# Two starting columns of the time shift written by GpSimd instead of VectorE, in a fused RWKV, attention and FP4 kernel

## The chip, the cores and the metric

The kernel runs on one core of one Trainium2 chip. The metric is the device time in microseconds (us) of one execution, as the median of several. The names in the profile are PE for TensorE (PEld is its weight load), DVE for VectorE, ACT for ScalarE, POOL for GpSimd and SP for the queue that issues the DMAs.

## The reference

The input x has 16 sequences of 512 tokens with 128 channels. Four parts are applied in a row, each on a layer norm of x and added to x: a stack of four RWKV layers, a gated FFN with FP4 quantised inputs and weights, a causal attention with one head of 64, and the same FFN again. The change lies in the RWKV layers:

```
for l in range(4):
    h = layernorm(x, ln1_w[l], ln1_b[l]);  hh = time_shift(h)
    k, v, sr = (mixes of h and hh) @ Wk, Wv, sigmoid(... @ Wr)
    x = x + (sr * wkv(time_decay, time_first, k, v)) @ Wo
    h = layernorm(x, ln2_w[l], ln2_b[l])
    hh = time_shift(h)                       # token t sees token t - 1, token 0 sees zeros
    xk = h * cmk[l] + hh * (1 - cmk[l])
    xr = h * cmr[l] + hh * (1 - cmr[l])
    x = x + sigmoid(xr @ Wcr) * (square(relu(xk @ Wck)) @ Wcv)
```

## The kernel before, in words

One sequence in one layer is a round: round r is layer r // 16 and sequence r % 16, and there are 64. Channels lie on the 128 partitions and the 512 tokens along the row, save for the layer norms, where 128 tokens lie on the partitions in four chunks. A round passes through some fifteen stages on five engines. Each engine has its own program, written as a loop over ticks; in tick t it works on the stages of several rounds, in an order that is written out by hand, and semaphores join the engines. In the steady part each engine does one piece of some fifteen rounds in one tick. The engines' ticks are not aligned in time: the tick numbers of two engines say nothing on which runs first.

The second time shift, of `h` after `ln2`, is built so. PE turns the normalised chunks (`turn2`, L1076), ACT writes `past`, the shifted term with its bias, for tokens 1 to 511 of both mixes (`keep_past`, L891), and DVE adds the unshifted term (`mix_k`, L420, and `mix_r`, L428). Column 0 of `past` has no token before it and depends on the layer alone; it is copied from the small tensor `cp`. `past` has two buffers, so the copy is made only in the first two rounds of each layer (`r % NB < 2`), 8 times in all, by `first_past` (L413). `mix_k` waits for it by the semaphore `pads`.

What stands around it: on DVE, in the order of the program, `scan_bb` (L374), `scan_aa` (L382), `gate` (L435), `sub_d` (L356), `variances` (L318, L319), `first_past`, `mix_k`, `mix_r`, in some rounds the preparation of a layer's weights (L253, L254), `mix_rt` (L332), `mix_v` (L339), `mix_t` (L325). The last three read two tensors in SBUF each. On POOL: `add_nd` (L692), `add_xb` (L708), `arg_r` (L685), `norm1_rest` (L659, three chunks of 128 columns), `rsqrts` (L651, a power, and L653, a product), `mul_y` (L697), `norm2_rest` (L659 again). On ACT, `tanh_c` (L912) waits for `add_xb`, and later in the tick `exp_d` (L853) writes what `scan_bb` reads.

Of the kernel before, what the change touches and what calls it, by code (L numbers as in the profile page):

```python
# [8 lines left out]
ALU = mybir.AluOpType  # L9
# [3 lines left out]
L, NB, T, C, F, I, D = 4, 16, 512, 128, 512, 352, 64  # L13
NT = T // 128
NR = L * NB
# [61 lines left out]
def hybrid_program(nc, x_in, weights, vecs, rows, fp4w, qkv, wout, mask, ident, out):  # L77
    ctx = ExitStack()
    with ctx:
# [28 lines left out]
        cw, cp, cz = [sb(k, [128, 2, L]) for k in ("cw", "cp", "cz")]  # L108
# [114 lines left out]
        def vector():  # L223
# [182 lines left out]
                    w.wait_ge(xa_done, r + 1)  # L406
                    stats(n_2, r, X[r % NB])

            def first_past(r):
                if 0 <= r < NR and r % NB < 2:  # L410
                    w.wait_ge(vecs_done, VECS)
                    w.wait_ge(xm_done, 2 * r - 2)
                    e.tensor_scalar(past[r % 2][:, :, 0:1], cp[:, :, r // NB:r // NB + 1], 1.0, 0.0, ALU.mult, ALU.add).then_inc(pads, 1)  # L413

            def mix_k(r):
                if 0 <= r < NR:
                    w.wait_ge(past_done, r + 1)
# [131 lines left out]
            for t in range(FIRST, TICKS):  # L549
                bn1(t - 1)  # L550
                add_xa(t - 7)
                mul_vs(t - 5)
                scan_bb(t - 5)
                scan_aa(t - 5)
                gate(t - 11)
                a_add(att_job(t - 6))
                scan_pp(t - 4)
                rwkv(t - 6)
                mul_up(ffn_job(t - 4), 0)
                fx_add(ffn_job(t - 2))  # L560
                mul_up(ffn_job(t - 4), 1)
                sub_d(t - 4)
                fx_sub(ffn_job(t - 2))
                fh_add(ffn_job(t - 5), 0)
                mul_up(ffn_job(t - 4), 2)
                fh_sub(ffn_job(t - 5), 0)
                bn2(t - 7)
                gated(t - 5)
                variances(t - 1)
                fx_scale(ffn_job(t - 1))  # L570
                mul_up(ffn_job(t - 4), 3)
                first_past(t - 8)
                init_stats(t + 1)
                mix_k(t - 8)
                mix_r(t - 8)
                prepare(t - 1)
                a_mask(att_job(t - 4), 0)
                fx_inverse(ffn_job(t - 1))
                fh_max(ffn_job(t - 4))
                a_max(att_job(t - 4), 0)  # L580
                weights_scales(t - 2)
                fh_scale(ffn_job(t - 4))
                fh_add(ffn_job(t - 5), 1)
                fh_inverse(ffn_job(t - 4))
                mix_rt(t - 3)
                init_affine(t)
                weights_rounded(t - 3)
                fh_sub(ffn_job(t - 5), 1)
                a_inverse(att_job(t - 5))
                a_mask(att_job(t - 4), 1)  # L590
                a_max(att_job(t - 4), 1)
                a_mask(att_job(t - 4), 2)
                a_max(att_job(t - 4), 2)
                mix_v(t - 3)
                mix_t(t - 3)
                a_mask(att_job(t - 4), 3)
                a_max(att_job(t - 4), 3)
                a_bn(att_job(t))
                f_bn(ffn_job(t + 3))
                fx_max(ffn_job(t))  # L600

        def gpsimd():
# [30 lines left out]
            def weights_divided(u):  # L633
                if u == 0:
                    w.wait_ge(q_steps, 3)
                    e.tensor_tensor(blocks(qw), blocks(qw), spread(wsc[:, 0, :], NQ // 16), ALU.mult).then_inc(q_y, 1)
# [25 lines left out]
            def norm1_rest(r):  # L662
                if 0 <= r < NR:
                    w.wait_ge(turned1, r - 1)
                    normalise(n_1, r, X[r % NB], z1[r % 2], 1, z1_rest)
# [33 lines left out]
            def scaled_p(r):  # L699
                if 0 <= r < NR:  # L700
                    w.wait_ge(p_done, r + 1)
                    w.wait_ge(seed_done, r + 1)
                    e.tensor_tensor(p[r % 2][:, :], p[r % 2][:, :], rc[r % 2][:, :], ALU.mult).then_inc(ps_done, 1)

            def add_xb(r):
                if 0 <= r < NR:
                    w.wait_ge(gate_done, r + 1)
                    e.tensor_tensor(X[r % NB][:, :], X[r % NB][:, :], cr[r % 2][:, :], ALU.add).then_inc(x_done, 1)  # L708
# [47 lines left out]
            for t in range(FIRST, TICKS):  # L756
                fx_divided(ffn_job(t - 4))
                scaled_p(t - 8)
                sub_dh1(t - 5)
                add_res(ffn_job(t + 1))  # L760
                fh_divided(ffn_job(t - 7), 0)
                fh_scaled(ffn_job(t - 8), 1)
                fh_divided(ffn_job(t - 7), 1)
                add_nd(t - 7)
                a_rsqrt(att_job(t - 3))
                add_xb(t - 13)
                arg_r(t - 6)
                f_rsqrt(ffn_job(t - 1))
                weights_divided(t - 5)
                norm1_rest(t - 4)  # L770
                fh_scaled(ffn_job(t - 7), 0)
                init_rsqrt(t - 1)
                fx_scaled(ffn_job(t - 4))
                rsqrts(t - 3)
                mul_y(t - 7)
                weights_scaled(t - 5)
                norm2_rest(t - 9)
                add_bias(att_job(t - 6))
# [649 lines left out]
```

## Time and profile before

| | us |
|---|---|
| median of 3 runs | 1329.43 (1328.66 to 1329.69) |
| profiled execution | 1329.69 |
| its span, first to last instruction | 1328.3 |
| PE busy | 1260.3 (95%) |
| DVE busy | 1221.2 (92%) |
| ACT busy | 1203.7 (91%) |
| POOL busy | 1170.1 (88%) |

The clock granted to TensorE is 0.993 of full speed in the mean. The RWKV layers take the span up to about 850 us, and the FFN and the attention what follows. A row of the timeline gives the start in us from the start of the span, the duration, the engine, the line, the operation with out<-in, how many instructions are merged (x3), and in brackets the idle time before it and what ended it. Starts are given to a hundredth of a microsecond; on one engine the next instruction starts up to 0.1 us before the recorded end of the one before it, so the distance from start to start is what an instruction takes of the engine.

### The profile page before, as it was taken

How to read it: one execution, taken by the hardware profiler on the slowest of the kernel's cores; microseconds unless marked ns; L12 is line 12 of the kernel's file. 1: busy time of each engine (PE TensorE's matmuls, PEld its weight loads, DVE VectorE, ACT ScalarE, POOL GpSimd, SP SyncE). 2: the span in 40 equal slices, each digit the busy share in tenths (PEclk: the TensorE clock that was granted, in tenths of full speed). 3: DMA queues.
4: the chain of work that ended last, by engine and by line, in shares of the span. 5: the costliest groups of instructions: out<-in, count | busy, mean ns of one | idle time of the engine just before them, and what ended most of it. 6: DMA issues, size and time to landing. Idle time of an engine off the chain costs nothing.

```text
span 1328.3 us, 23258 instructions
## 1 busy us (share of the span) xinstructions
PE 1260.3 (95%) x7177; PEld 919.8 (69%) x7177; DVE 1221.2 (92%) x2177; ACT 1203.7 (91%) x2283; POOL 1170.1 (88%) x1391
## 2 busy tenths in 40 slices
PE   2689999999999999999999999989999998999997
PEld 1346667777777777777777776766677786678776
DVE  7998999999999999999999999689998587988994
ACT  3789999999999999999999998977887899999874
POOL 6998999999999999999999998899988365756884
PEclk9899999999999999999999999999999999999999
DMA  6020000000000000000000000101000000000011
GB/s 184 1 78 1 1 17 1 1 1 1 1 1 1 1 1 1 1 1 1 1 1 1 1 1 25 32 25 28 5 2 1 1 1 1 1 17 17 25 32 41
DMA packets 26924, 18.54 MB, mean 14 GB/s; under 512 B 1072, under 2 KB 26160, under 8 KB 26800
## 3 DMA queue, kind: packets, MB, share of 16 engines
q1 hardware_dynamic: 26800, 17.05, 4.3%
q8 instruction: 58, 0.95, 0.3%
q14 instruction: 66, 0.54, 0.1%
HBM read 12.85 MB, written 4.19 MB: 13 GB/s over the span
## 4 chain that ended last, share of the span: by engine, by line
PE 32%; DVE 28%; issue 14%; ACT 13%; POOL 11%; DVEq 1%; DMA 0%; SPq 0%; ACTq 0%; POOLq 0%
PE ps L1256 5%; DVE ln_st L231 4%; PE ps L1235 4%; PE ps L1228 4%; DVE ab L382 4%; DVE now L365 3%; ACT now L863 3%; PE ps L1197 3%; PE ps L1306 2%; PE ps L1179 2%; PE ps L1244 2%; PE ps L1288 2%; DVE xv L339 2%; DVE xc L428 2%; DVE sr L332 2%
## 5 line engine op out<-in xcount | busy, mean ns | idle before, releaser
L1197 PEld LDWEIGHTS ps<-W,kf 128*128 128x128 f32 x2048 | 243.7, 192 | 31.0 <-issue 30.0
L1197 PE MATMUL ps<-W,kf 128*128 128x128 f32 x2048 | 248.8, 275 | 0.0
L1179 PE MATMUL ps<-xk,W 128*128 128x512 f32 x512 | 240.9, 593 | 0.0
L659 POOL TENSOR_SCALAR z<-X,ln_rs 128x128 f32<-128x128 f32 x384 | 170.1, 453 | 0.5 <-POOL ln_rs L653 0.4
L1179 PEld LDWEIGHTS ps<-xk,W 128*128 128x128 f32 x512 | 92.0, 191 | 89.5 <-issue 88.1
L899 ACT ACTIVATE kf<-ps 128x512 f32<-128x512 f32 x256 | 149.3, 585 | 2.8 <-PE ps L1179 2.7
L692 POOL TENSOR_TENSOR now<-now,ab 128x1024 f32<-128x1024 f32 x64 | 139.5, 2180 | 4.8 <-DVE ab L382 4.5
L906 ACT ACTIVATE kf<-kf 128x1024 f32<-128x1024 f32 x128 | 134.5, 1052 | 0.0
L743 POOL TENSOR_TENSOR W<-W,hsc 128x704 f32<-128x704 f32 x64 | 88.8, 1387 | 46.0 <-DVE W L510 45.8
L1076 PEld LDWEIGHTS ps<-idn,z 128*128 128x128 f32 x664 | 80.8, 143 | 67.3 <-issue 43.5
L1076 PE MATMUL ps<-idn,z 128*128 128x128 f32 x664 | 102.0, 277 | 18.0 <-POOL z L659 15.8
L651 POOL TENSOR_TENSOR ln_rs<-ln_rs,mhalf 128x8 f32<-128x8 f32 (+1 forms) x70 | 108.2, 1546 | 0.3 <-DVE ln_rs L319 0.2
L737 POOL TENSOR_TENSOR W<-W,hsc 128x704 f32<-128x704 f32 x64 | 88.7, 1387 | 15.2 <-DVE hsc L498 14.9
L1228 PE MATMUL ps<-WG,d 128*128 128x352 f32 x256 | 97.5, 463 | 0.7 <-ACT d L931 0.7
L1235 PE MATMUL ps<-WU,d 128*128 128x352 f32 x256 | 94.2, 470 | 3.7 <-DVE W L479 3.5
L231 DVE BATCH_NORM_STATS2 ln_st<-X 128x6 f32<-128x256 f32 x256 | 96.9, 420 | 0.4
L891 ACT ACTIVATE past<-ps,vec,cz 128x511 f32<-128x511 f32 x128 | 92.3, 777 | 1.3 <-PE ps L1076 1.3
L1186 PEld LDWEIGHTS ps<-W,xc 128*128 128x128 f32 x512 | 66.7, 191 | 33.4 <-ACT ps L838 18.2
L1165 PEld LDWEIGHTS ps<-W,rc 128*128 128x128 f32 x512 | 68.0, 194 | 30.4 <-issue 29.6
L697 POOL TENSOR_TENSOR now<-now,rc 128x512 f32<-128x512 f32 x64 | 83.3, 1301 | 4.0 <-ACT rc L871 3.9
L708 POOL TENSOR_TENSOR X<-X,cr 128x512 f32<-128x512 f32 x64 | 81.6, 1275 | 1.8 <-DVE cr L435 1.8
L374 DVE TENSOR_TENSOR_SCAN ab<-ps,now 128x512 f32<-128x512 f32 x64 | 77.9, 1217 | 5.3 <-ACT ps L853 5.2
(182 smaller groups left out, 3721.3 us busy)
## 6 DMA issues: line engine op xcount, KB each, us to landing
X<-x_in SPq DMA_DIRECT2D x16, 256.0 KB, 4.9
xi<-x_in SPq DMA_DIRECT2D x16, 256.0 KB, 2.9
out<-X SPq DMA_DIRECT2D x16, 256.0 KB, 2.3
W<-weights SPq DMA_DIRECT2D x4, 832.0 KB, 7.0
W<-fp4w SPq DMA_DIRECT2D x1, 560.0 KB, 7.5
row<-rows SPq DMA_DIRECT2D x1, 192.0 KB, 3.1
wqkv<-qkv SPq DMA_DIRECT2D x1, 96.0 KB, 5.4
idn<-ident SPq DMA_DIRECT2D x1, 64.0 KB, 3.2
```

The lines of the kernel that those rows point to most:

```text
L231: last = e.bn_stats(g.of(g.st, n)[:, 2 * k:2 * k + 2, :].rearrange("p a s -> p (a s)"), src[:, k * 256:(k + 1) * 256].rearrange("p (a c) - ...
L651: e.tensor_tensor(rs[:, 0, :], rs[:, 2, :], mhalf[:, 0:hi - lo], ALU.pow).then_inc(*own.next())
L659: last = e.tensor_scalar(chunk(dst, j), chunk(src, j), rs[:, 0, j:j + 1], rs[:, 1, j:j + 1], ALU.mult, ALU.add)
L692: e.tensor_tensor(now_sum[r % 2][:, 2:4, :], now_sum[r % 2][:, 2:4, :], ab[r % 2][:, :, 0:T], ALU.add).then_inc(nd_done, 1)
L891: last = e.activation(past[r % 2][:, k, 1:T], pT2[:, 0:T - 1], ACT.Identity, bias=v_of(r, LN2B), scale=cz[:, k, r // NB:r // NB + 1])
L899: e.activation(kf[r % 3][:, f, :], (pF0, pF1)[f % 2][:, :], ACT.Relu).then_inc(relu_done[f], 1)
L906: e.activation(both, both, ACT.Square).then_inc(sq_done[k], 1)
L1076: last = e.transpose(chunk(dst, j), chunk(src, j), idn[:, :])
L1179: e.matmul((pF0, pF1)[f % 2][:, :], w_of(r, WCK + f), xk[r % 2][:, :], start=True, stop=True).then_inc(kf_mm[f], 1)
L1197: last = e.matmul(chunk(pKV, j), kf[r % 3][:, f, j * 128:(j + 1) * 128], w_of(r, WCV + f), start=f == 0 and j == 0, stop=f == 3, skip_grou ...
L1228: e.matmul(pG[j % 2][:, 0:I], chunk(fx[n % 2], j), WG[:, :], start=True, stop=True).then_inc(g_mm, 1)
L1235: e.matmul(pU[j % 2][:, 0:I], chunk(fx[n % 2], j), WU[:, :], start=True, stop=True).then_inc(u_mm, 1)
```

## The change

`first_past` moves from DVE's program to POOL's. The instruction, its waits and its semaphore are the same. On DVE it stood between `variances` and `mix_k` of the same round. On POOL it stands ahead of `norm1_rest`, in the tick in which POOL also does `norm2_rest` of the same round.

```diff
 # vector
-            def first_past(r):
-                if 0 <= r < NR and r % NB < 2:
-                    w.wait_ge(vecs_done, VECS)
-                    w.wait_ge(xm_done, 2 * r - 2)
-                    e.tensor_scalar(past[r % 2][:, :, 0:1], cp[:, :, r // NB:r // NB + 1], 1.0, 0.0, ALU.mult, ALU.add).then_inc(pads, 1)
...
                 mul_up(ffn_job(t - 4), 3)
-                first_past(t - 8)
                 init_stats(t + 1)
 # gpsimd
+            def first_past(r):
+                if 0 <= r < NR and r % NB < 2:
+                    w.wait_ge(vecs_done, VECS)
+                    w.wait_ge(xm_done, 2 * r - 2)
+                    e.tensor_scalar(past[r % 2][:, :, 0:1], cp[:, :, r // NB:r // NB + 1], 1.0, 0.0, ALU.mult, ALU.add).then_inc(pads, 1)
...
                 weights_divided(t - 5)
+                first_past(t - 9)
                 norm1_rest(t - 4)
```

VectorE's program before, at round 16; `past<-cp` is `first_past`, `xk` and `xc` come from the two mixes:

```order
L319 TENSOR_SCALAR ln_rs<-ln_st 128x8
L413 TENSOR_SCALAR past<-cp 128x2 [waits s_xm]
L420 SCALAR_TENSOR_TENSOR xk<-ps,cw,past 128x512 [waits s_pads,s_kf_mm3,s_past]
L428 SCALAR_TENSOR_TENSOR xc<-ps,cw,past 128x512 [waits s_cr_mm]
L332 SCALAR_TENSOR_TENSOR sr<-dh,vec,h 128x512 [waits s_dh1,s_r_mm]
```

The same place after:

```order
L319 TENSOR_SCALAR ln_rs<-ln_st 128x8
L414 SCALAR_TENSOR_TENSOR xk<-ps,cw,past 128x512 [waits s_pads,s_kf_mm3,s_past]
L422 SCALAR_TENSOR_TENSOR xc<-ps,cw,past 128x512 [waits s_cr_mm]
L332 SCALAR_TENSOR_TENSOR sr<-dh,vec,h 128x512 [waits s_dh1,s_r_mm]
```

The copy is gone from between L319 and the first mix; the wait for `pads` stays and is now for another engine. (Some line numbers are 6 lower in the new file.)

GpSimd's program before, in the pass that has `norm2_rest` of round 16:

```order
L708 TENSOR_TENSOR X<-X,cr 128x512 [waits s_gate]
L685 TENSOR_SCALAR now<-d,capt 128x512 [waits s_rwkv,s_d]
L659 TENSOR_SCALAR z<-X,ln_rs 128x128 [waits s_turned1]
L659 TENSOR_SCALAR z<-X,ln_rs 128x128 x2
L651 TENSOR_TENSOR ln_rs<-ln_rs,mhalf 128x8 [waits s_ready]
L653 TENSOR_TENSOR ln_rs<-ln_rs 128x8 [waits s_gpsimd_steps]
L697 TENSOR_TENSOR now<-now,rc 128x512 [waits s_seed]
```

The same place after, where line numbers are 7 lower (L652 is the old L659, L644 the old L651):

```order
L707 TENSOR_TENSOR X<-X,cr 128x512 [waits s_gate]
L678 TENSOR_SCALAR now<-d,capt 128x512 [waits s_rwkv,s_d]
L702 TENSOR_SCALAR past<-cp 128x2 [waits s_xm]
L652 TENSOR_SCALAR z<-X,ln_rs 128x128 [waits s_turned1]
L652 TENSOR_SCALAR z<-X,ln_rs 128x128 x2
L644 TENSOR_TENSOR ln_rs<-ln_rs,mhalf 128x8 [waits s_ready]
L646 TENSOR_TENSOR ln_rs<-ln_rs 128x8 [waits s_gpsimd_steps]
L690 TENSOR_TENSOR now<-now,rc 128x512 [waits s_seed]
```

The copy now stands ahead of the three chunks, the power and the product, with a wait for the mixes of two rounds earlier. PE, ACT and SP have the same programs as before.

## Rows read from the trace of the kernel before

**Rows 1.** Windows. Stretch: length, busy PE, PEld, DVE, ACT, POOL; clock, DMA.

```profile
60.00:100.00 40.00, 33.55 (x121) 18.88 (x122) 38.04 (x65) 34.36 (x67) 38.72 (x51) 0.91 0.17 65
...
400.00:500.00 100.00, 99.99 (x571) 72.08 (x570) 99.72 (x165) 99.41 (x172) 99.37 (x114) 1.00 0.00 1
```

**Rows 2.** Timeline of DVE, rounds 15 and 16: start, duration, engine, line, operation.

```profile
274.94 0.16 DVE L319 TENSOR_SCALAR ln_rs<-ln_st 128x8 f32<-128x8 f32 x1
...
275.02 0.74 DVE L420 SCALAR_TENSOR_TENSOR xk<-ps,cw,past 128x512 f32<-128x512 f32 x1
...
276.34 0.73 DVE L332 SCALAR_TENSOR_TENSOR sr<-dh,vec,h 128x512 f32<-128x512 f32 x1
...
277.00 0.74 DVE L339 SCALAR_TENSOR_TENSOR xv<-dh,vec,h 128x512 f32<-128x512 f32 x1
...
287.28 0.16 DVE L413 TENSOR_SCALAR past<-cp 128x2 f32<-128x2 f32 x1
...
287.59 0.75 DVE L420 SCALAR_TENSOR_TENSOR xk<-ps,cw,past 128x512 f32<-128x512 f32 x1
...
290.24 0.75 DVE L325 SCALAR_TENSOR_TENSOR xt<-dh,vec,h 128x512 f32<-128x512 f32 x1
```

**Rows 3.** Timeline of POOL beside them: same columns.

```profile
275.00 1.30 POOL L659 TENSOR_SCALAR z<-X,ln_rs 128x128 f32<-128x128 f32 x3
...
276.27 1.64 POOL L651 TENSOR_TENSOR ln_rs<-ln_rs,mhalf 128x8 f32<-128x8 f32 x1
...
278.00 0.47 POOL L653 TENSOR_TENSOR ln_rs<-ln_rs 128x8 f32<-128x8 f32 x1
...
278.42 1.27 POOL L697 TENSOR_TENSOR now<-now,rc 128x512 f32<-128x512 f32 x1
...
290.26 0.79 POOL L653 TENSOR_TENSOR ln_rs<-ln_rs 128x8 f32<-128x8 f32 x1
```

**Rows 4.** Timeline of POOL in round 4: small operations, nothing held.

```profile
132.32 0.20 POOL L617 TENSOR_SCALAR in_rs<-in_st 128x4 f32<-128x4 f32 x1
...
132.61 0.23 POOL L618 TENSOR_SCALAR in_rs<-in_st 128x4 f32<-128x4 f32 x1
...
132.80 1.03 POOL L620 TENSOR_TENSOR in_rs<-in_rs,mhalf 128x4 f32<-128x4 f32 x1
...
136.27 0.20 POOL L653 TENSOR_TENSOR ln_rs<-ln_rs 128x8 f32<-128x8 f32 x1
```

**Rows 5.** Timeline of POOL and DVE in the first 32 us.

```profile
24.07 1.74 POOL L659 TENSOR_SCALAR z<-X,ln_rs 128x128 f32<-128x128 f32 x3
...
24.76 0.73 DVE L299 TENSOR_TENSOR xi<-xi,row 128x512 f32<-128x512 f32 x1
...
25.52 0.83 DVE L301 TENSOR_TENSOR X<-xi,row 128x512 f32<-128x512 f32 x1
...
27.04 0.75 DVE L283 TENSOR_SCALAR W<-W 128x1120 f32<-128x1120 f32 x1
...
27.06 1.62 POOL L620 TENSOR_TENSOR in_rs<-in_rs,mhalf 128x4 f32<-128x4 f32 x1
```

**Rows 6.** Timeline of ACT, DVE and POOL around round 29.

```profile
440.51 0.60 ACT L853 ACTIVATE ps<-ed 128x512 f32<-128x512 f32 x1
...
441.20 1.22 DVE L374 TENSOR_TENSOR_SCAN ab<-ps,now 128x512 f32<-128x512 f32 x1
...
445.79 1.28 POOL L708 TENSOR_TENSOR X<-X,cr 128x512 f32<-128x512 f32 x1
...
447.11 0.60 ACT L912 ACTIVATE cr<-ps 128x512 f32<-128x512 f32 x1
```

**Rows 7.** Timeline of DVE in round 19, where weights are prepared.

```profile
326.01 0.22 DVE L253 TENSOR_SCALAR W<-W 128x128 f32<-128x128 f32 x1
...
326.49 0.74 DVE L332 SCALAR_TENSOR_TENSOR sr<-dh,vec,h 128x512 f32<-128x512 f32 x1
```

## The prediction, made before the changed kernel ran

> **What bounds the kernel now.** I read the windows first, then the timeline of each engine over one tick, then the starts of one line from tick to tick. The windows show no single bound: between 400 and 500 us four engines are each busy over 99 of 100 us [rows 1]. So the question is which of them has slack hidden in its durations. DVE has none. Its instructions follow each other without idle time, and L420 comes every 12.26 us: the tick around round 16 is the exception, 287.59 − 275.02 = 12.57 us [rows 2]. There `first_past` starts at 287.28, and the mix behind it only 0.31 us later, since it waits for the copy's semaphore; elsewhere the mix follows L319 by 0.08 us (274.94 to 275.02).
>
> POOL does have slack, in L653. That product of 8 columns takes 0.20 us in round 4 [rows 4], 0.47 us in round 15 and 0.79 us in round 16 [rows 3]. Each time it ends just after DVE's L325: L325 runs from 290.24 to 290.99 [rows 2], L653 from 290.26 to 291.05. So a POOL instruction that starts inside one of DVE's operations with two inputs in SBUF (L332, L339, L325) is held to its end. POOL's free time per tick is 0.47 − 0.20 = 0.27 us, and its phase is pinned to DVE's.
>
> The Trainium skill has this as a rule (SBUF — State Buffer, Who interferes with whom): a DVE instruction with two SBUF inputs and a GpSimd instruction that reads SBUF exclude each other, whoever issues first keeping the ports for its whole instruction. The first half agrees with L653. By the second half L651, which starts at 276.27, 0.07 us ahead of L332, would hold L332 for over 1.5 us; the row of L332 shows 0.73 us. The sum below therefore has POOL held by DVE and DVE hardly by POOL.
>
> **What the change removes.** Six copies (rounds 16, 17, 32, 33, 48, 49) cost DVE 12.57 − 12.26 = 0.31 us each, 1.9 us in all; this is on the path, since every engine follows DVE's tick. In rounds 0 and 1 the copy has other work behind it and DVE is idle in part (38.04 of 40 us busy [rows 1]): nothing.
>
> **What it adds on POOL.** Nearest rows: L617 takes 0.20 us and the next starts 0.29 us after it, L618 0.23 us and 0.19 us [rows 4]. The row on the small side is the nearest in kind, so I take 0.20 us, bounds 0.16 (L653 less its overlap) to 0.29. Its wait is over long before: the mixes two rounds back end over 10 us earlier. The copy itself is done some 12 us before the mix that needs it, so the wait for `pads` costs DVE nothing.
>
> By durations alone 0.20 fits in 0.27 us. By phase it does not. L651 now starts at 276.27, L332 at 276.34: 0.07 us ahead. With the copy in front (POOL is back to back from L708 on) L651 starts at 276.47, inside L332, and is held to its end at 276.34 + 0.73 = 277.07. What a held power does is in [rows 5]: L620 starts at 27.06 inside L283, which ends at 27.79, and ends at 28.68, 0.89 us later, against 1.03 us free [rows 4]. So it needs its duration less 0.14 after the release. L651 (1.64 us [rows 3]) then ends at 277.07 + 1.50 = 278.57, L653 starts 0.09 later and leaves the engine after 0.16, and L697 starts at 278.82 against 278.42 [rows 3]: POOL is 0.40 us late, whatever the copy takes between 0.1 and 0.7 us.
>
> **Who waits for POOL.** L708 of the next pass is 0.40 late. L912 on ACT starts 0.04 us after L708 ends (447.07 to 447.11 [rows 6]), that is, it is already waiting for it; ACT then runs without a gap to L853. L853 ends at 441.11, DVE's L374 starts at 441.20 [rows 6]. Less the hand-over of 0.04 the slack is 0.05 us. So POOL's lateness reaches DVE less 0.05 us, two rounds after the held L651. Behind L374 stands everything of DVE's tick. PE, busy 99.99 of 100 us [rows 1], cannot catch up either: what it loses by ACT being late stays.
>
> Step by step, POOL late / DVE late: round 15: 0.40 / 0. Round 16, second copy: POOL is 0.60 late. The third chunk of L659, 0.43 before L651, would start 0.50 before L332, so it now starts 0.10 inside; held, it ends 0.32 us after the release ([rows 5]: 24.07 + 1.74 = 25.81, L299 ends at 25.49), and L651 falls into L339, 0.66 us on (277.00 − 276.34): 1.06 / 0. Round 17: DVE 0.35, POOL 0.71 later than DVE, again both held: 1.41 / 0.35. Round 18: DVE 1.06 − 0.05 = 1.01, POOL 0.40 later than DVE, L651 held by L332: 1.41 / 1.01. Round 19: DVE 1.36.
>
> From here the two can run in a loop. A held L651 puts POOL 0.40 behind DVE, DVE gets 0.35 of it two rounds on, and POOL enters the tick 0.05 to 0.35 later than its old phase. The old phase was 0.07 ahead of L332, so 0.05 is on the edge; but DVE pays too when POOL is in its way (L301 takes 0.83 us behind a held chunk [rows 5], 0.1 us more than L299 beside it), which widens the distance. I take it that the loop holds: 0.35 us per two rounds, 0.175 per round. It ends where DVE gets late by itself: in round 19 the weight preparation puts 0.48 us between L253 and L332 [rows 7], and POOL is ahead again. No preparation follows after round 19; next the loop ends about round 57, when the first norm and its power get shorter.
>
> **The sum**, against the profiled execution (1329.69; span 1328.3):
> - Layer 1: DVE 1.4 late at round 19, instead of 0.62 (two copies): +0.8.
> - Layers 2 and 3: 1.4 by round 35, 22 rounds at 0.175 = 3.9, the second pair of copies +1.0 (0.66 for the chunk and the power held one operation longer, 0.35 for one more step of the loop), less 4 × 0.31 = 1.25: +5.0.
> - Layer 0 with copies in rounds 0 and 1: 0. POOL's L617 is held there as well (the pattern of [rows 5]), which hides 0.2 us.
>
> Together +5.8: 1335.5, and 1335.2 on the scale of the median, which is 0.26 below the profiled run.
>
> **Rivals.**
> - *The slack hides the copy.* If a started power is not held by L332 (it has no row of its own starting inside it), POOL takes the 0.20 us out of the 0.27 in L653, and the six stalls are gone: −1.9, 1327.5. For it: all other ticks run 12.26 without a copy. Against it: every small POOL operation seen starting inside such a DVE operation is held, and L620 is a power too. 17%. This is the case on the other side; it decides at whether L651 may start after L332 has.
> - *Held, but it heals.* At the edge of 0.05 us POOL slips in ahead of L332 and the loop ends in each layer: +0.8 three times, +2.4, 1331.8; with the third chunk not held (a copy under 0.1 us) about 0. 28%.
> - *The loop holds*, my forecast: 4 to 8 us longer, 1333.5 to 1338. 43%.
> - *POOL misses its turn between L332 and L339.* Then each held L651 costs 1.06 instead of 0.40, up to 0.5 us per round, +13: 1342 or so. 12%.
>
> A measurement of this kernel can tell about 0.2% (2.7 us) from no change. The first rival and most of the second fall within it (0.35), a little of the first beyond it (0.04), the rest is slower (0.61). The range for 8 in 10 goes from the gain, 1327.4, to 1340, leaving out most of the last case. The forecast's own range is 1333.5 to 1338.
>
> **What would show it.** The copy on POOL at 0.2 us with no idle ahead. In round 15 L651 (now L644) of about 2.1 us where it had 1.64, L653's product back to 0.20, and L697 0.4 us later than before. Then idle ahead of DVE's L374 put down to ACT's L853, and of ACT's L912 put down to POOL. L420's distance: 12.26 in rounds 16 and 17 instead of 12.57, then 12.6 or more from round 17 to 19, and from round 35 on 12.3 to 12.6 in turn instead of a steady 12.26. I am wrong if L644 stays at 1.64 us with the copy ahead of it, or if the distance is 12.26 from round 36 on; in the first case the time falls by 1.9.

## The result, and the profile of the changed kernel

The changed kernel takes 1342.72 us (median of 4 runs, 1340.33 to 1348.81), the kernel before on the same chip 1329.56 (4 runs, 1328.66 to 1330.49): ratio 1.0106, 95% interval 1.0072 to 1.0141. It is slower, by 13.2 us (1.1%, clear of the interval), where 5.8 were forecast, and outside the forecast's range and the wider one. The profiled execution took 1343.09 us, with a span of 1341.8 (before: 1328.3), so 13.5 us are to be found in the trace.

The copy itself is as cheap as expected. All eight take 0.19 us, and nobody waits for them. Two windows of it answer to those of [rows 1]:

```profile
60.00:100.00 40.00, 33.44 (x120) 18.56 (x121) 37.43 (x62) 33.98 (x66) 38.55 (x53) 0.91 0.17 65
400.00:500.00 100.00, 98.99 (x563) 71.03 (x562) 99.62 (x163) 98.89 (x171) 99.10 (x115) 1.00 0.00 1
```

Layer 0 is nearly as it was: DVE is busy 37.43 us in the first window instead of 38.04, and the mix of round 15 starts at 275.24 instead of 275.02. Between 400 and 500 us PE fell from 99.99 to 98.99 us and ran 563 matmuls instead of 571, while DVE is as busy as before with fewer instructions (163 for 165). So a part of DVE's busy time is waiting inside its instructions, which no idle time shows. The page's list by groups says the same of POOL: its 70 powers are busy 108.2 us before (L651, 1546 ns each in the mean) and 114.2 us now (L644, 1632 ns), with hardly any idle time ahead (0.3 and 0.2 us in all).

Now the two rounds of the prediction. POOL, rounds 15 and 16 (start, duration):

```profile
275.32 0.19 POOL L702 TENSOR_SCALAR past<-cp 128x2 f32<-128x2 f32 x1
...
276.76 2.08 POOL L644 TENSOR_TENSOR ln_rs<-ln_rs,mhalf 128x8 f32<-128x8 f32 x1
278.92 0.20 POOL L646 TENSOR_TENSOR ln_rs<-ln_rs 128x8 f32<-128x8 f32 x1
279.08 1.29 POOL L690 TENSOR_TENSOR now<-now,rc 128x512 f32<-128x512 f32 x1
...
287.35 0.68 POOL L678 TENSOR_SCALAR now<-d,capt 128x512 f32<-128x512 f32 x1
...
288.29 3.30 POOL L652 TENSOR_SCALAR z<-X,ln_rs 128x128 f32<-128x128 f32 x3
...
293.45 1.27 POOL L690 TENSOR_TENSOR now<-now,rc 128x512 f32<-128x512 f32 x1
```

DVE beside it:

```profile
275.24 0.74 DVE L414 SCALAR_TENSOR_TENSOR xk<-ps,cw,past 128x512 f32<-128x512 f32 x1
...
276.56 0.77 DVE L332 SCALAR_TENSOR_TENSOR sr<-dh,vec,h 128x512 f32<-128x512 f32 x1
...
287.38 0.17 DVE L318 TENSOR_SCALAR ln_rs<-ln_st 128x8 f32<-128x8 f32 x1
287.46 0.60 DVE L319 TENSOR_SCALAR ln_rs<-ln_st 128x8 f32<-128x8 f32 x1
287.97 0.74 DVE L414 SCALAR_TENSOR_TENSOR xk<-ps,cw,past 128x512 f32<-128x512 f32 x1
...
289.29 0.74 DVE L332 SCALAR_TENSOR_TENSOR sr<-dh,vec,h 128x512 f32<-128x512 f32 x1
...
290.61 0.74 DVE L325 SCALAR_TENSOR_TENSOR xt<-dh,vec,h 128x512 f32<-128x512 f32 x1
```

Round 15 is the forecast: the power starts 0.20 us inside L332 (276.76 to 276.56), takes 2.08 us, the product is back at 0.20, and POOL is 0.44 late against DVE: L690 comes 3.84 us behind the mix, before 278.42 − 275.02 = 3.40 [rows 2, 3]. Round 16 is not. Two things stand in it that the prediction lacks. DVE's L319 takes 0.60 instead of 0.16 us: it ends at 288.06, just as POOL's L678 does (288.03). And the three chunks take 3.30 instead of 1.30 us; asked for alone, the third is this, to beyond the end of L325:

```profile
289.15 2.44 POOL L652 TENSOR_SCALAR z<-X,ln_rs 128x128 f32<-128x128 f32 x1
```

L690 then comes 5.48 us behind the mix: POOL is 2.1 late against DVE, which is itself 0.47 late in this round; 1.06 was forecast, and DVE on time.

The first of the two could have been foreseen. In round 7 of the kernel before, DVE's L318 takes 0.30 us instead of 0.18; it starts 0.41 inside POOL's L685 (174.36 to 175.04) and ends with it:

```profile
174.77 0.30 DVE L318 TENSOR_SCALAR ln_rs<-ln_st 128x8 f32<-128x8 f32 x1
```

Round 17, DVE; in brackets the idle time before, and what ended it:

```profile
294.13 1.23 DVE L374 TENSOR_TENSOR_SCAN ab<-ps,now 128x512 f32<-128x512 f32 x1 [0.38 <-ACT ps L853]
...
300.43 0.69 DVE L389 SCALAR_TENSOR_TENSOR p<-ps,now 128x512 f32<-128x512 f32 x1 [0.39 <-POOL now L685]
301.04 0.62 DVE L318 TENSOR_SCALAR ln_rs<-ln_st 128x8 f32<-128x8 f32 x1
...
301.64 0.74 DVE L414 SCALAR_TENSOR_TENSOR xk<-ps,cw,past 128x512 f32<-128x512 f32 x1
```

What released it, on POOL, and what POOL made late on ACT:

```profile
298.22 2.17 POOL L685 TENSOR_TENSOR now<-now,ab 128x1024 f32<-128x1024 f32 x1
300.36 1.26 POOL L707 TENSOR_TENSOR X<-X,cr 128x512 f32<-128x512 f32 x1
```

```profile
301.66 0.60 ACT L912 ACTIVATE cr<-ps 128x512 f32<-128x512 f32 x1 [1.54 <-POOL X L707]
```

The mix's distance is 301.64 − 287.97 = 13.67 us, 1.41 over the plain 12.26: from start to start 0.46 more in front of L374, 0.49 in front of L389, and 0.44 in L318, which ends 0.04 us after POOL's L707. So POOL's lateness reaches DVE by three ways, of which I had followed one (L374).

Later in the same round the third chunk, asked for alone, starts 0.30 us behind L332:

```profile
303.26 1.38 POOL L652 TENSOR_SCALAR z<-X,ln_rs 128x128 f32<-128x128 f32 x1
```

```profile
302.96 0.85 DVE L332 SCALAR_TENSOR_TENSOR sr<-dh,vec,h 128x512 f32<-128x512 f32 x1
```

It ends at 304.64, 0.16 us after the end of L339: two operations, where the forecast had one. L332 takes 0.85 instead of 0.73 us: when it started, the second chunk was still running on POOL (302.83 to 303.28).

In layer 3 a steady loop follows. The starts of the mix, with L339, L374 and L319 between them:

```profile
729.34 0.74 DVE L414 SCALAR_TENSOR_TENSOR xk<-ps,cw,past 128x512 f32<-128x512 f32 x1
742.21 0.74 DVE L414 SCALAR_TENSOR_TENSOR xk<-ps,cw,past 128x512 f32<-128x512 f32 x1
...
744.20 0.94 DVE L339 SCALAR_TENSOR_TENSOR xv<-dh,vec,h 128x512 f32<-128x512 f32 x1
...
748.51 1.23 DVE L374 TENSOR_TENSOR_SCAN ab<-ps,now 128x512 f32<-128x512 f32 x1 [0.32 <-ACT ps L853]
...
780.79 0.70 DVE L319 TENSOR_SCALAR ln_rs<-ln_st 128x8 f32<-128x8 f32 x1
781.41 0.74 DVE L414 SCALAR_TENSOR_TENSOR xk<-ps,cw,past 128x512 f32<-128x512 f32 x1
```

and POOL's chunks and power in it:

```profile
742.85 1.75 POOL L652 TENSOR_SCALAR z<-X,ln_rs 128x128 f32<-128x128 f32 x3
744.57 2.08 POOL L644 TENSOR_TENSOR ln_rs<-ln_rs,mhalf 128x8 f32<-128x8 f32 x1
...
780.79 0.68 POOL L678 TENSOR_SCALAR now<-d,capt 128x512 f32<-128x512 f32 x1
```

The tick is 12.87 us, 0.61 more than 12.26. POOL runs without idle and is held twice per tick, 0.45 us in the chunks (1.75 for 1.30) and 0.44 in the power (2.08 for 1.64); without the two it would need 11.98. DVE's 0.61 us lie in two places. From start to start 0.39 more stand in front of L374 (0.32 of it recorded as idle), and L339 takes 0.20 more, 0.94 instead of 0.74: it starts at 744.20, while the third chunk, which L332 had held, is running until 744.60. The loop ends in the row at 780.79: DVE's L319 is held for 0.54 us by POOL's L678, DVE falls back (13.46 us from the mix before to the next one), and the power starts together with L332 and is not held:

```profile
782.73 1.65 POOL L644 TENSOR_TENSOR ln_rs<-ln_rs,mhalf 128x8 f32<-128x8 f32 x1
```

```profile
782.73 0.76 DVE L332 SCALAR_TENSOR_TENSOR sr<-dh,vec,h 128x512 f32<-128x512 f32 x1
```

In layer 1 the end is of the same kind. In round 19 the power stands behind the preparation and is held all the same (it starts at 330.13, L332 at 329.85, and takes 2.08). One round on DVE, later by the preparation, puts its L318 inside POOL's L678 (340.60 to 341.28):

```profile
340.75 0.56 DVE L318 TENSOR_SCALAR ln_rs<-ln_st 128x8 f32<-128x8 f32 x1
```

After that the power is 0.07 ahead of L332.

The sum, from the mix's distances over the plain ones, round by round (the weight preparation's own 0.50 in round 20, which the kernel before has too, is taken off):

| layer | first copy round | next two | then, to the end of the loop | sum |
|---|---|---|---|---|
| 1 | 0.47 | 1.41 + 1.21 | 0.60 + 0.56 (0.40 of it L318 held) | 4.25 |
| 2 | 0.46 | 1.40 + 1.21 | 1.24 | 4.31 |
| 3 | 0.48 | 1.41 + 1.21 | 4 × 0.61 + 1.20 | 6.74 |

15.3 us in all. Less the six stalls of 0.31 that are gone this is 13.4, the 13.5 of the span. The runs of this kernel scatter over 8.5 us and those of the other over 2. Between the layers of this trace the loop takes 0 to 4 rounds at 0.6; that its length also differs from run to run, and makes the scatter, is likely but not shown, since one execution has a trace.

### The profile page after: what moved, and what is told of

It is laid out like the page before. It is cut to its first block, busy times and chain, and to the rows that moved or that the text cites. A ratio compares the mean times of both kernels' runs of the same rounds, so it can differ in the third digit from the quotient of the medians.

```text
span 1341.8 us, 23258 instructions
## 1 busy us (share of the span) xinstructions
PE 1263.8 (94%) x7177; PEld 920.0 (69%) x7177; DVE 1229.3 (92%) x2169; ACT 1204.3 (90%) x2283; POOL 1182.7 (88%) x1399
## 4 chain that ended last, share of the span: by engine, by line
PE 31%; DVE 24%; POOL 18%; issue 14%; ACT 11%; DMA 1%; DVEq 0%; SPq 0%; ACTq 0%; POOLq 0%
PE ps L1256 5%; PE ps L1235 4%; PE ps L1228 4%; POOL z L652 4%; DVE ab L382 3%; DVE ln_st L231 3%; PE ps L1197 3%; DVE now L365 3%; ACT now L863 2%; PE ps L1306 2%; PE ps L1179 2%; PE ps L1244 2%; POOL now L685 2%; PE ps L1288 2%; DVE xv L339 2%
## 5 line engine op out<-in xcount | busy, mean ns | idle before, releaser
L652 POOL TENSOR_SCALAR z<-X,ln_rs 128x128 f32<-128x128 f32 x384 | 182.7, 487 | 0.5 <-POOL ln_rs L646 0.4
L685 POOL TENSOR_TENSOR now<-now,ab 128x1024 f32<-128x1024 f32 x64 | 139.5, 2179 | 4.2 <-DVE ab L382 4.0
L644 POOL TENSOR_TENSOR ln_rs<-ln_rs,mhalf 128x8 f32<-128x8 f32 (+1 forms) x70 | 114.2, 1632 | 0.2 <-DVE ln_rs L319 0.2
L690 POOL TENSOR_TENSOR now<-now,rc 128x512 f32<-128x512 f32 x64 | 82.6, 1291 | 3.9 <-ACT rc L871 3.8
L374 DVE TENSOR_TENSOR_SCAN ab<-ps,now 128x512 f32<-128x512 f32 x64 | 77.9, 1217 | 8.8 <-ACT ps L853 8.7
L707 POOL TENSOR_TENSOR X<-X,cr 128x512 f32<-128x512 f32 x64 | 81.6, 1275 | 1.8 <-DVE cr L429 1.8
```

The costliest lines, as they stand in the source:

```text
L644: e.tensor_tensor(rs[:, 0, :], rs[:, 2, :], mhalf[:, 0:hi - lo], ALU.pow).then_inc(*own.next())
L652: last = e.tensor_scalar(chunk(dst, j), chunk(src, j), rs[:, 0, j:j + 1], rs[:, 1, j:j + 1], ALU.mult, ALU.add)
L685: e.tensor_tensor(now_sum[r % 2][:, 2:4, :], now_sum[r % 2][:, 2:4, :], ab[r % 2][:, :, 0:T], ALU.add).then_inc(nd_done, 1)
```

## Experiments

All times are medians; a ratio is to the kernel before, run in turn with it on the same chip (1329.65, 1329.29 and 1330.63 us beside the three groups of kernels); it is estimated from runs in turn and can differ a little from the quotient of the medians. "Distance" is that of DVE's first mix from one round to the next, over the plain 12.26.

**Without the later copies.** This gives the scale. The kernel leaves the copies out, so its results for the later layers are not right; the kernels built on it share that.

```diff
-                if 0 <= r < NR and r % NB < 2:
+                if 0 <= r < 2:
...
-                    w.wait_ge(pads, 2 * (r // NB) + min(r % NB, 1) + 1)      # in mix_k and mix_r
+                    w.wait_ge(pads, min(r, 1) + 1)
```

> The copies of rounds 16, 17, 32, 33, 48 and 49 are left out (column 0 keeps layer 0's values), those of rounds 0 and 1 stay on VectorE. Both theories: 6 x 0.31 = 1.9 us less than before, 1327.6; the mix every 12.26 us through rounds 16 and 17. It is the base for the kernels that add one thing on GpSimd.

Measured: 1327.61 us (1326.80 to 1328.75, 11 runs), ratio 0.9984 [0.9975, 0.9993], 2.0 us less. The copies on DVE cost what the 0.31 of [rows 2] says, and no more can be won here.

**The copy on DVE, but earlier.** It stands behind `sub_d`, and starts 1.3 us earlier than in [rows 2].

```diff
                 sub_d(t - 4)
+                first_past(t - 8)
...
-                first_past(t - 8)
```

> The copy stays on VectorE and stands right behind sub_d, ahead of fx_sub, bn2, gated and variances; GpSimd has its old program. Theory of the port (a GpSimd operation that arrives inside L332, L339 or L325 is held, and the rest of the loss follows from that): GpSimd and its phase are untouched, VectorE pays 0.08 us per copy instead of 0.38, so 6 x 0.3 = 1.8 us less than before (1327.7), distance of the mix in rounds 16 and 17 about 12.33. Rival, the wait: the mix's wait for the copy costs 0.31 us wherever the copy stands, then no change against before (1329.5).

Measured: 1333.87 us (6 runs), ratio 1.0030 [1.0018, 1.0042]: 4 us slower, not 2 faster. DVE of this kernel:

```profile
285.98 0.77 DVE L413 TENSOR_SCALAR past<-cp 128x2 f32<-128x2 f32 x1
...
287.93 0.38 DVE L318 TENSOR_SCALAR ln_rs<-ln_st 128x8 f32<-128x8 f32 x1
```

and POOL:

```profile
285.46 1.27 POOL L708 TENSOR_TENSOR X<-X,cr 128x512 f32<-128x512 f32 x1
```

The copy of two columns takes 0.77 us, until 0.02 after POOL's L708 has ended (286.73), and L318 0.38, until 0.04 after a chunk of POOL (L659, 287.82 to 288.28) has. The distances are 0.90 and 0.83 over instead of 0.31, which makes 3.3 of the 4.2 us; the rest lies outside the copy rounds. POOL's power stays at 1.65 us. So a short DVE `tensor_scalar` can be held by a running POOL operation, and this costs time with POOL's power never held. The theory that the wait of 0.31 was the only cost of the copy on DVE fell.

**Only the first copy of each layer on POOL.**

```diff
-                if 0 <= r < NR and r % NB < 2:      # on DVE
+                if 0 <= r < NR and r % NB == 1:
...
+                if 0 <= r < NR and r % NB == 0:      # on POOL
```

> As the changed kernel, but only the copy of each layer's first round is on GpSimd; that of the second round is on VectorE as before. Theory of the port: in round 15 the power is held (2.08 us) and GpSimd is 0.44 late; in round 16 GpSimd's L685 (its min/max on d) holds VectorE's small L319 for 0.45 us, and with no second copy that puts VectorE behind GpSimd again: it heals at once, at 0.46 + 0.31 per layer instead of 0.62, so +0.5 us against before (1330). Rival, the load: each copy on GpSimd costs a like amount, so half of the changed kernel's loss, +6 to +7 us (1336).

Measured: 1335.79 us (4 runs), ratio 1.0045 [1.0030, 1.0060]. I had expected one copy to heal at once; it does not. POOL in round 16, which has no copy ahead of it there:

```profile
290.29 3.56 POOL L651 TENSOR_TENSOR ln_rs<-ln_rs,mhalf 128x8 f32<-128x8 f32 x1
```

DVE beside it:

```profile
290.28 0.73 DVE L332 SCALAR_TENSOR_TENSOR sr<-dh,vec,h 128x512 f32<-128x512 f32 x1
...
291.61 0.73 DVE L325 SCALAR_TENSOR_TENSOR xt<-dh,vec,h 128x512 f32<-128x512 f32 x1
```

The power starts 0.01 us behind L332 and is released only when L325 ends (292.34), after three operations: 3.56 us. Started 0.20 us behind, in round 15, it was released after one. The distances of rounds 16 and 17 are 0.47 and 1.88 over; in round 17 DVE is itself held twice, in L318 and in the copy that it still has, 0.61 and 0.68 us, and so comes out behind POOL again. By layers 0.47 + 1.88, 0.46 + 1.99, 0.47 + 1.87: 7.1. The six distances of the kernel before make 1.9, so 5.3 us are in these rounds; the spans of the two profiled executions differ by 5.5 (1333.8 and 1328.3), the medians by 6.1.

**Single copies, far apart** (of spare columns, so that nothing waits for them; the kernel without later copies otherwise).

```diff
+                if NB <= r < NR and r % NB in (0, 4):      # spare_copy, on POOL
+                    e.tensor_scalar(scr[...], cp[:, :, r // NB:r // NB + 1], 1.0, 0.0, ALU.mult, ALU.add)
```

> Built on the kernel without later copies (column 0 keeps layer 0's values); GpSimd gets six spare copies of the same shape at the place of the change, in rounds 0 and 4 of layers 1 to 3 instead of 0 and 1. Theory of the port: each heals in one round at 0.46 us (one held L319), the copy of round 20 even less since the weight preparation of round 19 gives way: +2.3 to +2.8 against the kernel without copies, 1330. Rival, the load: six copies cost what six copies cost, +15 against the kernel without copies (1342).

Measured: 1346.29 us (1342.28 to 1350.36, 4 runs), ratio 1.0123 [1.0100, 1.0145]. Six copies, four rounds apart, cost at least as much as together (the intervals of the two ratios overlap). Five of the six give 0.47, then a power of 3.56 us, then 1.06 to 1.69 more; behind two of them rounds of 12.87 follow (one in layer 1, four in layer 3). The copy of round 20 adds only 0.24.

**One copy in the whole kernel**, in front of the chunks in the pass of DVE's round 39.

```diff
+                if r == 40:      # spare_copy, on POOL
```

> Built on the kernel without later copies; one spare copy on GpSimd at the place of the change, for round 40, far from any other event. Theory of the port: in round 39 the power takes 2.08 us and the product is 0.44 late; in round 40 L319 is held for 0.45 us; then healed: +0.46, 1328.1. Rival, the loop as I forecast it (0.35 us per two rounds to round 57): +3 us, 1331.

Measured: 1333.13 us (1330.26 to 1339.39, 8 runs), ratio 1.0034 [1.0017, 1.0051]. Neither number was right (the rival's 1331 lies among the runs, its 0.35 per two rounds in no row), and the scatter is the result. The profiled execution is the one of 1339.39. In round 39 its power takes 2.08, as forecast; one round on:

```profile
583.66 3.56 POOL L657 TENSOR_TENSOR ln_rs<-ln_rs,mhalf 128x8 f32<-128x8 f32 x1
```

One instruction of 0.19 us is followed by distances of 0.47, 1.05 and then sixteen times 0.60 over, up to round 57: some 11 us. The fastest run is about 3 us above the kernel without the copy; it has no trace, so that its loop was shorter is inferred from the time.

**A memset instead of the copy, at the change's place**, of the same two columns, about 0.1 us.

```diff
+                spare_set(t - 9)      # e.memset(scr[...], 0.0), on POOL
                 norm1_rest(t - 4)
```

> The same memset (0.1 us, write only), but at the place of the change, ahead of the three chunks and the power. Theory of the port: it puts the power's start from 0.07 ahead of L332 to 0.03 inside it, so the power is held (2.2 us) and the same chain follows as with the copy: +4 to +15 against the kernel without copies. If the power slips in, the edge lies above 0.03 and the time is 1327.6. Rival, the load: the same as the kernel with the memset between power and product, whatever that is.

Measured: 1327.68 us (10 runs), ratio 0.9987 [0.9978, 0.9996], as without it. POOL of round 15:

```profile
274.60 0.12 POOL L647 MEMSET scr<- 128x2 f32 x1
...
275.96 1.66 POOL L656 TENSOR_TENSOR ln_rs<-ln_rs,mhalf 128x8 f32<-128x8 f32 x1
```

and DVE:

```profile
275.98 0.74 DVE L333 SCALAR_TENSOR_TENSOR sr<-dh,vec,h 128x512 f32<-128x512 f32 x1
```

The power (L656 here) starts 0.02 us in front of L333, the old L332, and is not held. Nine powers in the kernels with one copy on POOL per layer, with copies far apart and with a single copy start 0.01 us behind it, and each takes 3.56. So the edge lies near equal starts, but the order of the starts alone does not settle it: in the changed kernel's row at 782.73 the power starts no earlier than L332 and takes 1.65, and in the kernel with copies far apart one that starts 0.01 behind takes 1.64 (at 554.3).

**The memset between power and product.**

```diff
                     e.tensor_tensor(rs[:, 0, :], rs[:, 2, :], mhalf[:, 0:hi - lo], ALU.pow).then_inc(*own.next())
+                    spare_set(s - 6)
                     w.wait_ge(*own.so_far())
```

> Built on the kernel without later copies (column 0 keeps layer 0's values); GpSimd gets a memset of two columns (0.1 us, it writes SBUF and reads none) between the power L651 and the product L653 in rounds 16, 17, 32, 33, 48, 49. Theory of the port: L653 is waiting for the end of L325 there anyway, so its held time shrinks by 0.1 and nothing moves: the time of the kernel without copies, 1327.6. Rival, the load (every piece of extra GpSimd time in these ticks starts the slow loop): 4 us or more.

Measured: 1327.58 us (10 runs), ratio 0.9988 [0.9978, 0.9997]: nothing. But the trace shows that this is not because POOL waits for a turn there. In round 15 the memset runs from 278.50 to 278.61, in the 0.08 us that lie between power and product anyway, and the product behind it takes 0.47 us, as without it; so this kernel puts nothing on POOL and does not test the slack. What it shows beside that: the memset, which reads nothing, starts inside DVE's L326 (the old L325, 278.29 to 279.03) and is not held, while the product is.

**The copy between power and product.** The changed kernel, with only the place on POOL another.

```diff
-                first_past(t - 9)
...
+                    first_past(s - 6)      # between L644 and L646
```

> The changed kernel with the copy on GpSimd moved between the power and the product. Theory of the port: the copy arrives inside L325 and is held to its end, the product leaves 0.17 us late, the next pass's power starts 0.1 inside L332 and is held: 0.44 late one round later than in the changed kernel, and then the second copy: a loss again, +2 to +13 against before. Rival, the slack (0.27 us in the product's wait takes a copy of 0.19 us): 1.9 us less than before (1327.6).

Measured: 1328.82 us (10 runs), ratio 0.9998 [0.9988, 1.0007]. The loss of 13 us is gone by the place alone. POOL:

```profile
277.18 0.45 POOL L703 TENSOR_SCALAR past<-cp 128x2 f32<-128x2 f32 x1
...
286.02 0.68 POOL L679 TENSOR_SCALAR now<-d,capt 128x512 f32<-128x512 f32 x1
```

DVE a round later:

```profile
286.28 0.44 DVE L318 TENSOR_SCALAR ln_rs<-ln_st 128x8 f32<-128x8 f32 x1
```

The copy takes the product's wait, 0.45 us, and POOL is about 0.17 late. DVE's L318 then waits for L679 (0.44 for 0.16 us, to 286.72; L679 ends at 286.70). The distance is 0.26 over: DVE is set back as far as POOL, the power stays 0.07 in front of L332, and nothing follows. The gain of 1.9 is spent on it (6 × 0.27 = 1.6). Both expectations missed: the power is not held, and the copy is not free.

**The changed kernel, with DVE later by as much.** If it is the order at L332 and not the work that costs, more work on DVE must make this kernel faster.

```diff
                 mix_r(t - 8)
+                spare_stats(t - 7)      # bn_stats of 128x256 constants, if NB <= r < NR and r % NB < 2
```

> The changed kernel, with more work put back on DVE: a statistics operation over 128x256 constants (two of them take 0.75 us in the trace, so about 0.34 start to start) is issued behind the second mix of the last round before each copy round and of the first copy round (rounds 15, 16, 31, 32, 47, 48), into scratch that nobody reads. It stands ahead of L332, so that L332 starts about 0.34 us later in the very rounds in which POOL is 0.19 late by its copy; the power is then again ahead of L332. Theory of the order (the loss comes from the power operation arriving behind L332's start, not from the work on POOL): the 13 us go away and only the added DVE work is paid: 1327.6 (the time without these copies) plus 6 times 0.34 = 1329.7, range 1329 to 1331; the power stays at 1.65 us and the distances of rounds 16, 17, 32, 33, 48, 49 show +0.3 and 0. Rival, load: POOL's 0.19 us more is what costs, and DVE's work comes on top: 1342 or more. Rival, the small DVE operation (L319) caught by POOL's L678 is the start of it: it depends on the two engines' distance, which here shrinks by 0.15 against the kernel before, so it would still be caught in some rounds: 1330 to 1333.

Measured: 1332.93 us (1331.95 to 1334.10, 11 runs), ratio 1.0017 [1.0008, 1.0025]: 2.3 us over the kernel before instead of 13.2. DVE does more than in the changed kernel and POOL the same, and 11 us are gone, with the scatter. POOL:

```profile
278.33 1.65 POOL L651 TENSOR_TENSOR ln_rs<-ln_rs,mhalf 128x8 f32<-128x8 f32 x1
...
288.83 0.69 POOL L685 TENSOR_SCALAR now<-d,capt 128x512 f32<-128x512 f32 x1
```

DVE:

```profile
278.12 0.42 DVE L413 BATCH_NORM_STATS2 scr<-row 128x6 f32<-128x256 f32 x1
278.46 0.73 DVE L333 SCALAR_TENSOR_TENSOR sr<-dh,vec,h 128x512 f32<-128x512 f32 x1
...
289.22 0.32 DVE L319 TENSOR_SCALAR ln_rs<-ln_st 128x8 f32<-128x8 f32 x1
```

The power is 0.13 us in front of L333 and takes 1.65. A round costs 0.46 to 0.47, not 0.34: L319 (the old L318) is held for 0.13 by L685, to 289.54 against 289.52. The order theory named 1329 to 1331, which beside a kernel before of 1330.6 instead of 1329.65 is 1330.0 to 1332.0; the time is outside. The hold of L319 accounts for 0.8 us (six times 0.13). By the distances the six rounds cost 2.8 us against 1.9 in the kernel before, so 0.9 of the 2.3 us; the rest is not in the copy rounds. In the profiled execution DVE is 1.8 us later than in the kernel before at round 15 already (276.80 against 275.02), ahead of the first added operation, which is not explained. The second rival, L319 caught by POOL as the start of the loss, named 1330 to 1333, and the time fits it; but in the trace L319 is caught in all six rounds (0.30 to 0.32 us) and no loss follows behind them. Load as the cause is excluded: it named 1342 or more.

**Three more places for the copy**: SP's queue, ACT, and DVE two small operations earlier. On SP the copy is a DMA with semaphores of its own, and the DMAs of the later layers' weights stand behind the first two of them.

```diff
+                    e.dma_start(past[r % 2][:, :, 0:1], cp[:, :, r // NB:r // NB + 1], ...)   # SP
```

> The kernel before, with column 0 of the mix's second operand written by a DMA of SP's queue, from the prepared vector, instead of by DVE; no engine spends anything on it, and the slot is free a round (12 us) before the mix reads it. Expected as without the later copies: 1327.6 (1.9 less than before), the six first rounds of layers 1 to 3 at the plain period. It is real work, with its result used. Rival: the mixes wait for the DMA, which moves 256 pieces of 4 bytes: if it takes over about 10 us, each of the six rounds loses what is above that; from this kernel's other DMAs (2 to 5 us) it should not.

Measured: 1328.91 us (11 runs), ratio 0.9984 [0.9975, 0.9993]. That is 1.7 us less than before. A DMA lands after 1.9 us (median of 8), and the distances show nothing.

```diff
+                first_past(t - 8)      # on ACT, e.activation(..., ACT.Copy)
                 tanh_c(t - 9)
```

> The kernel before, with the copy on ACT in front of its tanh L912, behind the activation that writes the other columns. ACT runs without a gap there in rounds 15 and 16 (the activation ends 274.38, the tanh starts 274.37), so it makes ACT 0.2 us late, and DVE is 0.31 earlier. Theory that a chain through ACT decides: ACT's two arguments, its Relu and exponentials follow 0.2 late; DVE's scan L374 waits for ACT's L853 with 0.05 to spare, so 0.15 to 0.25 a copy round shows, 6 times: 1327.6 + 1.2 = 1328.8, range 1327.4 to 1330. Rival: ACT's lateness reaches POOL over L912 and the gate, and pushes the power behind L332's start: 1333 to 1345.

Measured: 1328.90 us (11 runs), ratio 0.9986 [0.9977, 0.9995]. Also nothing, against the 0.15 to 0.25 a round that I expected. ACT:

```profile
287.92 0.22 ACT L905 ACTIVATE past<-cp 128x2 f32<-128x2 f32 x1
288.04 0.60 ACT L911 ACTIVATE cr<-ps 128x512 f32<-128x512 f32 x1
```

The tanh L911 comes 1.45 us after the start of the first of the two activations ahead of it (286.59), without the copy 1.43. In both kernels it starts 0.03 us after POOL's add ends (286.60 to 286.63 before, 288.01 to 288.04 here): it waited about 0.1 us there for POOL, though no idle time is recorded, and the copy lies in that.

```diff
+                first_past(t - 8)      # on DVE
                 variances(t - 1)
```

> The kernel before, with the copy still on DVE, two small operations earlier (in front of L318 and L319 instead of behind them). Of the 0.31 us that a copy costs, the time to the mix is a wait for its semaphore; the two small operations (0.17 to 0.20 start to start) would lie inside it. Expected: a copy costs 0.12 to 0.2 instead of 0.31, so 1327.6 + 6 x 0.15 = 1328.5, range 1327.8 to 1329.2. Rival from the copy put much earlier (held 0.77 us by POOL's running operation): L678 on POOL starts at 286.58 in round 16 and has ended by 287.25, the copy comes at 287.11 and would be held until then, 0.14 more: the time is then as before or up to 1 us above.

Measured: 1329.15 us (11 runs), ratio 0.9987 [0.9978, 0.9996]. Distances 0.17 to 0.18 over, as forecast: the wait for the copy's semaphore is half covered by L318 and L319.

## Why the prediction was wrong

**Right.** The copy's price (0.19, forecast 0.20), the removed stalls (0.31 each), the power pushed into L332 and its size (2.08, forecast 2.1), the 0.40 of the first round (0.44) [rows 3], the way over ACT to L374 (0.38 idle, 0.32 in the loop), and next to nothing in layer 0 [rows 1]. The loop of layer 1 ends at the time forecast, but not as forecast: the preparation of round 19 [rows 7] did not bring the power in front of L332 in its own round (2.08 us at 330.13), L318 held in round 20 did. The direction was that of the likeliest case.

**The first term that failed: "The third chunk ... held, it ends 0.32 us after the release", one operation on.** It was let go after three (3.30 us against 1.30), so POOL was 2.1 late instead of 1.06. I had priced a missed turn between L332 and L339 as a rival, at 12%, and took [rows 5], where a held instruction gets in behind L299, as the rule. The rows give several lengths: a power 0.20 behind L332 is released after one operation, a chunk 0.30 behind after two (round 17), a power 0.01 behind after three, and a chunk that had begun 0.14 before L332 also after three, while a power that begins 0.02 or 0.07 before it loses none. What decides between one and three is not shown. The distance is one candidate. Another is what ran before: wherever, from round 15 on, a power or chunk got in after one operation, an earlier chunk of POOL was still running when that operation began, and made it longer (L332 0.75 to 0.85, L339 0.94, L325 0.77; so it was in round 17 too, where it took two). In the nine rounds with a power of 3.56 us L332 takes its plain 0.73 to 0.74. The two were not separated. For the two that start before L332 my reading is that the chunk still has its columns to read when L332 comes and the power has read its eight; the runs show the two outcomes, not the reads.

**The second: "the sum below therefore has POOL held by DVE and DVE hardly by POOL".** A running power does not hold L332, a running chunk lengthens L332 and L339 by up to 0.2 us (0.20 per round of the loop), and a small `tensor_scalar` operation of DVE is held to the end of POOL's operation. In the rows shown such an operation, started while POOL works, ended 0.02 to 0.04 us after POOL's operation: 0.30 in the kernel before, 0.60 in round 16, 0.62 in round 17, 0.56 in round 20, 0.70 at the end of the loop, 0.77 for the early copy, 0.44 and 0.32 in the last two. (One that starts 0.03 us behind POOL's may still pass: L318 at 287.38 took 0.17.) The Trainium skill says this (SBUF — State Buffer, Who interferes with whom): copies and `tensor_scalar` of DVE can take both port pairs if their operands allow it, and whoever issues first keeps the shared one for the whole instruction. I had weighed that second half against L332 alone and let it go as a whole. By the durations above it is right for the small operations; by [rows 2, 3] a power that has started does not hold L332 (0.73 us).

**What the two did to the sum.** Rounds 16 to 18 cost DVE 3.1 us per layer (0.47 + 1.41 + 1.21); the prediction had 0, 0.35 and 0.66, so 1.0. Three layers: 9.3 against 3.0. That is 6.3 of the 7.6 us missing. Round 16 is L319 held, round 17 the three ways of which I had followed one, round 18 the late POOL once more (L318 is held for 0.61 again).

**The third: the loop, "0.175 per round".** Where it runs it takes 0.61, since POOL is held in two places and becomes the engine that sets the tick; the slack of 0.05 does not come into it. But it does not run from round 35 to 57. It ended in round 35 in layer 2 and in round 55 in layer 3, in a way that I had not seen: DVE's L319 caught by POOL's L678. The prediction had 4.7 us for all after the third round of each layer, and 6.0 were measured, in other rounds. It is near the right size for a wrong reason, which is luck.

**The rivals.** "The slack hides the copy" is refuted in its place, since the power was held, and half true two instructions further on: between power and product the copy lies in the wait of the product, and each still costs 0.27 us through L318. "Held, but it heals" needs DVE to be set back as far as POOL; this happened only in that kernel, by L318, and not at the change's place. "POOL misses its turn" gave +13 and 1342, which is the time measured, but in part by luck: its price was for the power, and no power of the changed kernel takes more than 2.08 us. Only chunks missed turns, in the round of each layer's second copy and in the one after it, and the rival had nothing on the holds of L318 and L319.

**Open.** What the loss would be without the hold of DVE's L318 and L319 was not tried, so the share of each of the two mechanisms is not separated; the kernel with DVE later removes the held power and shortens the hold of the small operation (0.32 instead of 0.60) at once. How a loop ends can be read, though: in its 26 rounds at 0.6 in three traces (here, copies far apart, single copy) L319 starts 0.02 to 0.05 us before POOL's L678, as at 742.13 and 742.18, and is not held; in the rounds that end it before the layers do (35 and 55 here, 19 with the copies far apart) L319 starts up to 0.02 behind and takes 0.70 to 0.74. So a shift of some hundredths of a microsecond decides whether the loop ends or takes another round. What makes the shift, in round 35 in one layer, in round 55 in another, and not before round 57 behind the single copy, is not shown.

## What to carry to other kernels

Where two engines hold each other and run in step, as DVE and POOL do here, ask of each moved instruction on which side of the partner's next operation it puts the ones behind it; its own 0.2 us tell little, the same copy costs 0, 0.27 or more than 2 us by its place. Before a small operation goes to an engine beside such a pair, look for one that takes no part in it: here a DMA or ACT did the copy for next to nothing and gave 1.7 us of the 2.0 that leaving it out gives. And a price for "held" needs its length in partner operations: look for rows of both kinds of release, and price the long one.

## What the runs showed that was not expected

- A power on POOL that starts 0.01 us behind the first of three DVE operations in a row was released after the third in nine rows, 3.56 us instead of 1.65, and not held at all in one. With 0.20 us it is released after the first, 2.08. What decides is open.
- A DVE operation on 2 or 8 columns takes up to 0.92 us (the early copy in round 0) instead of 0.16 when it starts while a POOL operation runs, and ends 0.02 to 0.08 us after it.
- One instruction of 0.19 us cost 11 us in one execution, and some 3 us in another of the same kernel: 1330.26 to 1339.39.
- An instruction of 128x2 on ACT in front of one that waits 0.1 us costs 0.02 us, and on POOL 0.27 in the wait of another.
